# Four-pass window attention: masks that start before the score products are complete, and a new order of the PSUM copies

## Chip, core and metric

One core of one Trainium2 chip. The metric is the device time of one execution of the whole program in microseconds, the median of the runs taken.

## The reference, cut to what matters

The program is a chain of four layers over activations of 4 sequences x 1024 positions x 256 channels: a linear attention, a block of two local-attention layers with their feed-forward parts, a gated attention, and a ternary-weight feed-forward. The block of two layers stands in the program twice, so its attention part runs four times ("passes", `run` = 0 to 3). The change touches only this part:

```python
h = shift_token(x)                       # half of the channels one position later
q, k, v = split(h @ wqkv, 3)             # 8 heads of 64
q = l2norm(q) * qs;  k = l2norm(k) * ksc
q, k = rotary_xpos(q, k)
sim = q_window @ k_window^T              # 128 queries against their own and the previous 128 keys
sim = where(mask, -max, sim);  attn = softmax(sim)
x = x + (attn @ v_window) @ wo
```

## The kernel before

**Tiles and slots.** A pass works on 32 tiles of 128 positions (NT = 32). It is a software pipeline: in slot T each engine does its part of several tiles at once. T+3 is loaded, transposed and multiplied with the q and k weights, T+2 with the v weights, q and k of T+1 are turned (transposed) for the scores, T itself goes through scores, masks, exponentials and the transposition of the probabilities, T-1 through the products with V, T-2 through the output projection. The order of the steps within a slot is written out by hand for each engine in its function `slot`. Four slots (u = T mod 4) make an iteration; the first and last iterations are unrolled and the middle ones are a hardware loop. Engines are tied together by counting semaphores alone: every step waits for a count and adds one.

**TensorE** (`slot`, line 567): `sc_` (32 small score products in eight rounds, L508), `pv_` of T-1 (L544), `wo_` of T-2, `tr_` q of T+1 (four transposes, L478), `v_` of T+2 (six products, L363 to L365), `ht` of T+3 (two transposes, L419 and L420), `pt_` of two groups of heads (L521 to L523), `tr_` k of T+1 (L478), `qk_` q of T+3, two more `pt_`, `qk_` k of T+3.

**ScalarE** (`slot`, line 1264): the square of k (L1224), eight exponentials with row sums (`sc_`, L1247), the copy `OT_hi` of the numerator of T-1 (`ot_`, L1262), then the copies out of PSUM: qT (L1238), V (L1231), hT_hi (L1217), two probT (L1255), kT (L1238), the square of q, two more probT.

**VectorE** (`slot`, line 1921): the sum of squares of q (L1867), eight masks with running minimum (`sc_`, L1893, one per head, announced once for each pair of heads), the reciprocal of the first four sums (L1900), the rotation of k (L1853 to L1855), the second reciprocal, the normalising of k of the next tile (`norm_`, L1873), hT_lo (L1833), the sum of squares of k, `OT_lo` (L1905), the residual (L1910), the rotation of q.

**GpSimd** (`slot`, line 2718): the sums of the rotated halves (L2693), four products of probabilities with reciprocals (`pn_`, L2699), the inverse root of the norms (`pow_`, L2684 and L2686).

**SyncE** issues the loads of H (of tile T+4), the copies of V's halves and the stores; it is not changed.

**PSUM.** Banks 0 and 1 take q and k of T+3, bank 1 also the transposes of H; bank 5 takes v of T+2 and then the turned k of T+1, so the turning of k waits until ScalarE has copied V. Banks 2 to 4 are the scores and then the turned probabilities; banks 6 and 7 (`pair_bank`) the numerators in their lower halves, the projection in the upper half of bank 7.

The lines the reasons touch: `ht` waits for the reader of bank 1 (`k_read`, L417 and L418), `tr_` for V (`v_read(T + 1)`, in the branch of j = 1), `qk_` of T+3 for hT_lo (`s_dvHT`). In run 0 VectorE and GpSimd also normalise the residual stream of later tiles in the slots u = 1 to 3 (`extra`).

Of the kernel before, what the change touches and what calls it, by code (L numbers as in the profile page):

```python
# [94 lines left out]
def build(nc, a, out):  # L95

    ctx = ExitStack()
    with ctx:
# [169 lines left out]
        def gate_weight(x, i, n=1):  # L268
# [32 lines left out]
        s_dvQN, s_peS, s_peSB = sem("s_dvQN"), sem("s_peS"), sem("s_peSB")  # L301
# [22 lines left out]
                      *s_acKT, s_peS, s_peSB, *s_dvMX, *s_acEX, *s_plPN, *s_pePT, *s_acPT, *s_pePV, *s_dvRS,  # L324
# [12 lines left out]
        def input_bank(run, T):  # L337
            return bank[2 + T] if spare(run, T) else bank[1]
# [11 lines left out]
        def tensor_program(e):  # L350
# [36 lines left out]
            def pass_A(run, ffn_first):  # L387
# [25 lines left out]
                def ht(T, u):  # L413
# [3 lines left out]
                    if not spare(run, T) and not (isinstance(T, int) and T == 0):  # L417
                        k_read(T - 1)  # L418
# [13 lines left out]
                def qk_(T, u, j):  # L432
# [48 lines left out]
                def sc_(T, u):  # L481
# [7 lines left out]
                    for n, (odd, even, piece) in enumerate(SCORE_ORDER):  # L489
# [3 lines left out]
                        for half_ in range(2):  # L493
                            for h in (odd, even):
# [31 lines left out]
                def pv_(T, u):  # L526
# [18 lines left out]
                    for hf in range(2):  # L545
                        for x in (2, 3):
                            for g in range(2):
                                for i in range(2):
                                    product(2 * hf + g, i, x, slice(DH * i, DH * i + DH), hf == 0 and x == 2)
                    for hf in range(2):  # L550
                        for i in range(2):
                            for x in (0, 1):
                                for g in range(2):
                                    ins = product(2 * hf + g, i, x, slice(0, P), False)
                        ins.then_inc(s_pePV[hf], 1)
# [11 lines left out]
                def slot(T, u):  # L567
# [2841 lines left out]
```

## Time and profile before

| what | us |
|---|---|
| median of 3 runs | 3214.93 (3213.61 to 3220.47) |
| the profiled execution's own time | 3218.03 |
| its span, first to last instruction | 3216.0 |
| TensorE matmul busy | 3018.5 (94%) |
| VectorE busy | 2361.8 (73%) |
| ScalarE busy | 1721.1 (54%) |
| GpSimd busy | 1671.5 (52%) |
| granted TensorE clock, mean | 0.993 |

A busy matmul is counted from its start to its modelled end, and matmuls overlap, so TensorE's 94% hides waits: they are seen as steps between the starts of instructions. The four attention passes take about 390 us each.

### The profile page before, as it was taken

The page shows a single profiled execution, that of the slowest core. Times are in us where ns is not written, and L with a number is a line of the kernel's source. Part 1 is how long each engine was busy: PE and PEld are TensorE (multiplying, and loading weights), DVE is VectorE, ACT ScalarE, POOL GpSimd, SP SyncE. Part 2 cuts the span into 40 slices and gives each one's busy share as a digit, 9 for nine tenths or more (in the row PEclk, how much of TensorE's full clock was granted, in tenths as well). Part 3 has the DMA queues.
Part 4 walks back from the last instruction along what each step waited for, and adds up shares of the span by engine and source line. Part 5 has one row for each costly group of instructions (what it writes and reads, how often), then busy time and mean ns, then how long its engine had stood idle before and what let it go on. Part 6 is the DMA issues. An engine that isn't in the chain of part 4 may idle for free.

```text
span 3216.0 us, 98899 instructions
## 1 busy us (share of the span) xinstructions
PE 3018.5 (94%) x35586; PEld 2604.5 (81%) x35586; DVE 2361.8 (73%) x6543; ACT 1721.1 (54%) x4532; POOL 1671.5 (52%) x1839
## 2 busy tenths in 40 slices
PE   6999989989999999999899999999999899999889
PEld 4777878878887888998688878877888788898778
DVE  6777777677777786777677777767777688777766
ACT  4666652266667324665676763237666622454445
POOL 7777740077777224323777771037777444317610
PEclk9999999999999999999999999999999999999999
DMA  4211121021111101000211112102111200100001
GB/s 146 58 42 39 38 81 36 23 62 39 37 38 37 45 20 42 10 11 21 57 39 37 38 37 78 29 25 66 37 38 35 66 26 13 27 1 1 1 14 39
DMA packets 178773, 122.82 MB, mean 38 GB/s; under 512 B 27532, under 2 KB 175336, under 8 KB 178024
## 3 DMA queue, kind: packets, MB, share of 16 engines
q1 hardware_dynamic: 177432, 117.77, 13.6%
q8 instruction: 147, 2.41, 0.3%
q10 hardware_dynamic: 1104, 1.90, 0.2%
q14 instruction: 90, 0.74, 0.1%
HBM read 48.29 MB, written 20.98 MB: 22 GB/s over the span
## 4 chain that ended last, share of the span: by engine, by line
PE 62%; ACT 18%; issue 8%; DVE 8%; DMA 1%; POOL 1%; DVEq 1%; SPq 0%; ACTq 0%; POOLq 0%
ACT prob L1247 14%; PE bank L363 7%; PE bank L365 5%; PE scores L508 5%; PE bank L364 5%; PE scores L363 4%; PE scores L364 4%; PE scores L365 4%; PE bank L478 2%; PE pair_bank L770 2%; PE pair_bank L769 2%; PE pair_bank L768 2%; ACT V L1231 2%; PE scores L714 2%; PE scores L713 2%
## 5 line engine op out<-in xcount | busy, mean ns | idle before, releaser
L2699 POOL TENSOR_TENSOR prob<-prob,rsum 128x384 f32<-128x384 f32 x512 | 467.5, 933 | 282.6 <-DVE rsum L1900 267.2
L1247 ACT ACTIVATE prob<-prob,nmax 128x192 f32<-128x192 f32 x1024 | 452.0, 443 | 290.5 <-DVE nmax L1893 290.4
L1440 ACT ACTIVATE gate<-scores,bias 128x512 f32<-128x512 f32 x192 | 132.2, 689 | 511.4 <-PE scores L365 511.4
L2686 POOL TENSOR_TENSOR rn<-ss,mhalf 128x16 f32<-128x16 f32 x128 | 375.2, 2931 | 10.7
L363 PE MATMUL bank<-wqkv_hi,hT_hi 128*128 128x512 f32 x768 | 338.9, 441 | 8.7 <-DVE hT_lo L1833 3.7
L2693 POOL TENSOR_TENSOR qk<-rot_t 128x512 f32<-128x512 f32 x256 | 322.6, 1278 | 36.1 <-DVE ss L1867 29.7
L2667 POOL TENSOR_TENSOR rstd<-meanvar,eps 128x4 f32<-128x4 f32 x48 | 11.1, 231 | 627.2 <-DVE meanvar L1825 627.2
L1893 DVE CUSTOM_DVE_ANT_0 prob<-scores,masks,rn 128x192 f32<-128x192 f32 x768 | 267.7, 412 | 84.4 <-PE scores L508 83.9
L365 PE MATMUL bank<-wqkv_hi,hT_lo 128*128 128x512 f32 x768 | 305.7, 398 | 0.0
L364 PE MATMUL bank<-wqkv_lo,hT_hi 128*128 128x512 f32 x768 | 302.5, 394 | 0.0
L1853 DVE TENSOR_TENSOR rot_t<-bank,rot 128x512 f32<-128x512 f32 x256 | 176.1, 688 | 163.8 <-ACT qk L1224 156.2
L1224 ACT ACTIVATE qk<-bank 128x512 f32<-128x512 f32 x256 | 152.5, 597 | 221.8 <-PE bank L365 221.8
L363 PE MATMUL scores<-gT_hi,w_hi 128*128 128x512 f32 x576 | 227.5, 395 | 2.5 <-issue 1.7
L508 PEld LDWEIGHTS scores<-kT,qT 64*64 64x64 f32 x8192 | 184.6, 134 | 53.3 <-issue 53.3
L364 PE MATMUL scores<-gT_lo,w_hi 128*128 128x512 f32 x576 | 226.3, 393 | 0.0
L1255 ACT ACTIVATE probT<-scores 128x384 f32<-128x384 f32 x512 | 222.0, 488 | 6.2 <-PE scores L523 6.0
L365 PE MATMUL scores<-gT_hi,w_lo 128*128 128x512 f32 x576 | 224.3, 389 | 0.0
L478 PE MATMUL bank<-misc,qk 128*128 128x128 f32 x1024 | 158.3, 277 | 64.2 <-ACT V L1231 53.9
L508 PE MATMUL scores<-kT,qT 64*64 64x128 f32 (+1 forms) x8192 | 202.0, 248 | 8.3 <-ACT probT L1255 8.3
L363 PEld LDWEIGHTS bank<-wqkv_hi,hT_hi 128*128 128x128 f32 x768 | 145.6, 190 | 57.3 <-DVE hT_lo L1833 29.9
L1247 ACT ACTIVATION_READ_ACCUMULATOR prob<-prob,nmax 128x1 f32 x1024 | 191.5, 187 | 0.0
L478 PEld LDWEIGHTS bank<-misc,qk 128*128 128x128 f32 x1024 | 112.9, 141 | 92.9 <-DVE qk L1873 74.6
(338 smaller groups left out, 9662.6 us busy)
## 6 DMA issues: line engine op xcount, KB each, us to landing
Vlo<-V SPq DMA_DIRECT2D x256, 64.0 KB, 2.0
Vhi<-V SPq DMA_DIRECT2D x256, 64.0 KB, 2.0
H<-Y SPq DMA_DIRECT2D x128, 64.0 KB, 1.8
H<-ya SPq DMA_DIRECT2D x128, 64.0 KB, 1.9
yb<-Y SPq DMA_DIRECT2D x128, 64.0 KB, 1.6
HB<-Y SPq DMA_DIRECT2D x32, 256.0 KB, 2.8
HB<-yb SPq DMA_DIRECT2D x32, 256.0 KB, 3.0
raw<-in_L_ffn_wqkv SPq DMA_DIRECT2D x4, 1536.0 KB, 6.9
```

The costliest lines, as they stand in the source:

```text
L363: e.matmul(o, lh, rh, start=start, stop=False)
L364: e.matmul(o, lh, rl, start=False, stop=False)
L365: return e.matmul(o, ll, rh, start=False, stop=stop)
L478: i = e.transpose(o[:, c * P:(c + 1) * P], half(u, j)[:, c * P:(c + 1) * P], identf)
L508: ins = e.matmul(o, queries, keys, start=opens, stop=True, skip_group_check=True)
L1247: ins = e.activation(pb, pb, ACT.Exp, bias=nm[r][:, x:x + 1], scale=-1.0, accum_out=sums[r][:, x:x + 1])
L1255: e.activation(PTs[gi][:, :], b_[:, 0:2 * KW], ACT.Copy).then_inc(s_acPT[gi], 1)
L1853: e.tensor_tensor(o1_, x_, tab(2 * j, 0, DH), ALU.mult)
L1893: ins = e.tensor_tensor_reduce(Pb[gi][:, w], scores[:, s0:s0 + KW], m[:, DH:] if i == 0 else m[:, 0:KW], rn[u][:, h:h + 1], BIG, ALU.add, ...
L2686: e.tensor_tensor(rn[u][:, :], ss[:, :], mhalf[:, :], ALU.pow).then_inc(s_plRN, 1)
L2693: e.tensor_tensor(half(u, j), t1[:, w], t2[:, w], ALU.add).then_inc(s_plAD[j], 1)
L2699: e.tensor_tensor(pair, pair, rs[:, 2 * gi:2 * gi + 2].unsqueeze(2).to_broadcast([P, 2, KW]), ALU.mult).then_inc(s_plPN[gi], 1)
```

## The change

It touches the attention pass in six ways.

1. Heads are grouped anew (PAIRS, TURN_BANK), and a new semaphore `s_peSA` tells of the fifth of eight score rounds. VectorE masks heads 4 and 6 after that signal, then waits for the whole of the scores (`s_peS`) and masks the other six. All four waits for the turned probabilities (`s_pePT`) now stand ahead of the first mask. Each mask is announced by itself, and ScalarE's exponentials wait for a single mask each.
2. ScalarE's copy of the numerator (`ot_`) moves from behind the exponentials to behind kT, so qT, V, hT and two probT come ahead of it.
3. TensorE transposes H (`ht`) ahead of the turning of q and of v, not behind them, and into the unused upper half of bank 6. The wait for the reader of bank 1 moves from `ht` to the product of k (`qk_`, j = 1). `pv_` and ScalarE's `ot_` get a wait for hT_lo (`s_dvHT`), since bank 6 is shared.
4. VectorE normalises k of T+1 right behind the first reciprocal, ahead of the rotation of k and of the second reciprocal.
5. The groups of heads are turned, scaled and multiplied in the order 0, 1, 2, 3; `s_pePV[n]` now stands for groups n and n+2, with the waits to match.
6. GpSimd's waits on the masks count two for each tile.

```diff
-PAIRS = [(0, 4), (1, 5), (2, 6), (3, 7)]
+PAIRS = [(0, 4), (2, 6), (1, 5), (3, 7)]
+EXP_ORDER = (((0, 1), (1, 1), (0, 0), (1, 0)), ((2, 0), (3, 0), (2, 1), (3, 1)))
-TURN_BANK = (3, 2, 2, 4)
+TURN_BANK = (2, 3, 4, 2)
@@ input_bank
-            return bank[2 + T] if spare(run, T) else bank[1]
+            if spare(run, T):
+                return bank[2 + T]
+            return bank[1] if isinstance(T, int) and T < 3 else bank[6][:, 2 * P:4 * P]
@@ TensorE, ht and qk_
-                    if not spare(run, T) and not (isinstance(T, int) and T == 0):
+                    if run == DEPTH and isinstance(T, int) and 1 <= T < 3:
                         k_read(T - 1)
-                    elif j == 1 and spare(run, T):
+                    elif j == 1 and (not early or spare(run, T)):
                         k_read(T - 1)
@@ TensorE, sc_
+                                if half_ == 1 and h == 0 and piece == 0:
+                                    ins.then_inc(s_peSA, 1)
@@ TensorE, pt_
-                    if gi == 1:
-                        e.wait_ge(s_dvMX[2], G + 1 + OFF)
-                    if gi == 2:
-                        e.wait_ge(s_acPT[1], G + 1 + OFF)
+                    if gi == 0:
+                        e.wait_ge(s_dvMX[2], 2 * G + 2 + OFF)
+                        e.wait_ge(s_dvMX[3], 2 * G + 2 + OFF)
+                    if gi == 3:
+                        e.wait_ge(s_acPT[0], G + 1 + OFF)
@@ TensorE, pv_
+                    if inside(T + 3):
+                        e.wait_ge(s_dvHT, G + 4 + OFF)
@@ TensorE, slot
+                    if inside(T + 3):
+                        ht(T + 3, (u + 3) % U)
                     if inside(T + 1):
                         tr_(T + 1, (u + 1) % U, 0)
                     if inside(T + 2):
                         v_(T + 2, (u + 2) % U)
-                    if inside(T + 3):
-                        ht(T + 3, (u + 3) % U)
                     if inside(T):
+                        pt_(T, u, 0)
                         pt_(T, u, 1)
-                        pt_(T, u, 0)
@@ ScalarE, sc_
-                    e.wait_ge(s_dvMX[gi], G + 1 + OFF)
-                    for i in range(2):
+                    for n, (gi, i) in enumerate(EXP_ORDER[hf]):
                         x = 2 * gi + i
                         pb = Pb[gi][:, i * KW:(i + 1) * KW]
-                        ins = e.activation(pb, pb, ACT.Exp, bias=nm[r][:, x:x + 1], scale=-1.0, accum_out=sums[r][:, x:x + 1])
-                    ins.then_inc(s_acEX[gi], 1)
+                        e.wait_ge(s_dvMX[gi], 2 * G + 1 + n // 2 + OFF)
+                        e.activation(pb, pb, ACT.Exp, bias=nm[r][:, x:x + 1], scale=-1.0, accum_out=sums[r][:, x:x + 1]).then_inc(s_acEX[gi], 1)
@@ ScalarE, ot_
+                    if inside(T + 4):
+                        e.wait_ge(s_dvHT, G + 5 + OFF)
@@ ScalarE, slot
-                    if inside(T - 1):
-                        ot_(T - 1, (u - 1) % U)
                     if inside(T + 1):
                         tr_(T + 1, (u + 1) % U, 0)
...
                     if inside(T + 1):
                         tr_(T + 1, (u + 1) % U, 1)
+                    if inside(T - 1):
+                        ot_(T - 1, (u - 1) % U)
@@ VectorE, sc_
-                    e.wait_ge(s_peS, G + 1 + OFF)
+                    e.wait_ge(s_peSA, G + 1 + OFF)
                     e.sem_inc(s_passed, 1)
                     e.wait_ge(s_plRN, 2 * G + 2 + OFF)
                     e.sem_inc(s_passed, 1)
-                    e.wait_ge(s_pePT[gi], G + OFF)
-                    e.sem_inc(s_passed, 1)
+                    for g in range(NG):
+                        e.wait_ge(s_pePT[g], G + OFF)
+                        e.sem_inc(s_passed, 1)
...
-                    for i in range(2):
+                    for n, (gi, i) in enumerate(EXP_ORDER[0] + EXP_ORDER[1]):
+                        if n == 2:
+                            e.wait_ge(s_peS, G + 1 + OFF)
+                            e.sem_inc(s_passed, 1)
@@ VectorE, slot
                         rs_(T, u, 0)
+                    if inside(T + 1):
+                        norm_(T + 1, (u + 1) % U, 1)
                     if inside(T + 2):
                         qk_(T + 2, (u + 2) % U, 1)
                     if inside(T):
                         rs_(T, u, 1)
-                    if inside(T + 1):
-                        norm_(T + 1, (u + 1) % U, 1)
```

## Rows read from the trace of the kernel before

**Rows 1.** Windows, one slot each: us, busy by engine (count), clock, DMA share, GB/s

```profile
858.06:870.78 12.72, 12.12 (x182) 10.00 (x181) 9.05 (x32) 8.52 (x27) 9.19 (x9) 1.00 0.15 36
895.38:907.69 12.31, 11.75 (x181) 9.91 (x180) 9.09 (x32) 8.52 (x27) 9.38 (x9) 1.00 0.16 37
270.12:283.63 13.51, 11.94 (x182) 9.93 (x181) 11.24 (x36) 8.52 (x27) 10.08 (x10) 1.00 0.21 53
```

**Rows 2.** Waits, whole span: waiter <- releaser, us in total, times, longest

```profile
PE bank L478 <- ACT V L1231: 53.9, 115, 0.8
...
PE bank L419 <- DVE rot_t L1855: 30.0, 40, 4.3
PEld bank L363 <- DVE hT_lo L1833: 29.9, 117, 0.7
```

**Rows 3.** Timeline of TensorE: start, us, what, xcount, idle before

```profile
845.76 1.57 PE L508 MATMUL scores<-kT,qT 64*64 64x128 f32 x64
847.16 0.34 PE L544 MATMUL pair_bank<-probT,Vlo 64*64 64x64 f32 x8
...
851.97 0.40 PE L365 MATMUL bank<-wqkv_hi,hT_lo 128*128 128x512 f32 x1
852.21 0.28 PE L419 MATMUL bank<-misc,H 128*128 128x128 f32 x1
...
852.43 0.27 PE L521 MATMUL scores<-misc,prob 128*128 128x128 f32 x1
...
853.80 0.63 PE L478 MATMUL bank<-misc,qk 128*128 128x128 f32 x4 [0.55 <-ACT V L1231]
854.43 0.50 PE L363 MATMUL bank<-wqkv_hi,hT_hi 128*128 128x512 f32 x1
...
858.06 1.57 PE L508 MATMUL scores<-kT,qT 64*64 64x128 f32 x64
859.69 0.34 PE L544 MATMUL pair_bank<-probT,Vlo 64*64 64x64 f32 x8
...
872.28 0.34 PE L544 MATMUL pair_bank<-probT,Vlo 64*64 64x64 f32 x8
```

**Rows 4.** Timeline of ScalarE, the same slot

```profile
848.59 0.46 ACT L1247 ACTIVATE prob<-prob,nmax 128x192 f32<-128x192 f32 x1 [2.12 <-DVE nmax L1893]
...
852.12 0.58 ACT L1262 ACTIVATE OT_hi<-pair_bank 128x512 fp32r<-128x512 f32 x1
852.60 0.58 ACT L1238 ACTIVATE qT<-bank 128x512 f32<-128x512 f32 x1
853.07 0.58 ACT L1231 ACTIVATE V<-bank 128x512 f32<-128x512 f32 x1
853.55 0.37 ACT L1217 ACTIVATE hT_hi<-bank 128x256 fp32r<-128x256 f32 x1
...
854.55 0.60 ACT L1238 ACTIVATE kT<-bank 128x512 f32<-128x512 f32 x1
856.12 0.60 ACT L1224 ACTIVATE qk<-bank 128x512 f32<-128x512 f32 x1 [0.96 <-PE bank L365]
```

**Rows 5.** Chain of waits ahead of the first mask, the same slot (DVEq: VectorE's queue)

```profile
847.40 0.02 DVEq L1880
...
847.52 0.02 DVEq L1882
...
847.79 0.23 DVE prob L1893
```

**Rows 6.** Timeline of VectorE and GpSimd, the same slot

```profile
850.50 0.17 DVE L1900 RECIPROCAL rsum<-sums 128x4 f32<-128x4 f32 x1
...
852.43 0.69 DVE L1873 TENSOR_TENSOR qk<-qk,rn 128x512 f32<-128x512 f32 x1
...
850.75 0.83 POOL L2699 TENSOR_TENSOR prob<-prob,rsum 128x384 f32<-128x384 f32 x1 [2.17 <-DVE rsum L1900]
...
852.50 1.30 POOL L2699 TENSOR_TENSOR prob<-prob,rsum 128x384 f32<-128x384 f32 x1
```

More of the change, by code:

```diff
@@ L544, in product @@
                         return e.matmul(bank[6 + i][cols, o0:o0 + DH], keys[x][rows, h * DH:(h + 1) * DH], PTs[gi][rows, p0:p0 + DH], start=start, stop=x < 2, skip_group_check=True)
-                    for hf in range(2):
+                    for n in range(2):
                         for x in (2, 3):
-                            for g in range(2):
+                            for gi in (n, n + 2):
                                 for i in range(2):
-                                    product(2 * hf + g, i, x, slice(DH * i, DH * i + DH), hf == 0 and x == 2)
-                    for hf in range(2):
+                                    product(gi, i, x, slice(DH * i, DH * i + DH), n == 0 and x == 2)
+                    for n in range(2):
                         for i in range(2):
                             for x in (0, 1):
-                                for g in range(2):
-                                    ins = product(2 * hf + g, i, x, slice(0, P), False)
-                        ins.then_inc(s_pePV[hf], 1)
+                                for gi in (n, n + 2):
+                                    ins = product(gi, i, x, slice(0, P), False)
+                        ins.then_inc(s_pePV[n], 1)
                 def wo_(T, u):
@@ L587, in slot @@
                     if inside(T):
+                        pt_(T, u, 2)
                         pt_(T, u, 3)
-                        pt_(T, u, 2)
                     if inside(T + 3):
@@ L1253, in pt_ @@
                     e.wait_ge(s_pePT[gi], G + 1 + OFF)
-                    e.wait_ge(s_pePV[gi // 2], G + OFF)
+                    e.wait_ge(s_pePV[gi % 2], G + OFF)
                     e.activation(PTs[gi][:, :], b_[:, 0:2 * KW], ACT.Copy).then_inc(s_acPT[gi], 1)
@@ L1267, in slot @@
                     if inside(T):
+                        sc_(T, u, 0)
                         sc_(T, u, 1)
-                        sc_(T, u, 0)
-                        sc_(T, u, 3)
-                        sc_(T, u, 2)
-                    if inside(T - 1):
-                        ot_(T - 1, (u - 1) % U)
                     if inside(T + 1):
@@ L1287, in slot @@
                     if inside(T):
+                        pt_(T, u, 2)
                         pt_(T, u, 3)
-                        pt_(T, u, 2)
                 def iteration(it):
@@ L1873, in norm_, with sc_ @@
                     e.tensor_tensor(heads(half(u, j)), heads(half(u, j)), rn[u][:, j * HEADS:(j + 1) * HEADS].unsqueeze(2).to_broadcast([P, HEADS, DH]), ALU.mult).then_inc(s_dvQN, 1)
-                def sc_(T, u, gi):
+                def sc_(T, u):
                     G = R0 + T
@@ L1892, in sc_ @@
                         s0 = SCORE_AT[h]
-                        ins = e.tensor_tensor_reduce(Pb[gi][:, w], scores[:, s0:s0 + KW], m[:, DH:] if i == 0 else m[:, 0:KW], rn[u][:, h:h + 1], BIG, ALU.add, ALU.min, nm[r][:, x:x + 1])
-                    ins.then_inc(s_dvMX[gi], 1)
+                        e.tensor_tensor_reduce(Pb[gi][:, w], scores[:, s0:s0 + KW], m[:, DH:] if i == 0 else m[:, 0:KW], rn[u][:, h:h + 1], BIG, ALU.add, ALU.min, nm[r][:, x:x + 1]).then_inc(s_dvMX[gi], 1)
                 def rs_(T, u, hf):
                     G = R0 + T
-                    e.wait_ge(s_acEX[2 * hf], G + 1 + OFF)
-                    e.wait_ge(s_acEX[2 * hf + 1], G + 1 + OFF)
+                    e.wait_ge(s_acEX[2 * hf], 2 * G + 2 + OFF)
+                    e.wait_ge(s_acEX[2 * hf + 1], 2 * G + 2 + OFF)
                     e.reciprocal(rs[:, 4 * hf:4 * hf + 4], sums[u % 2][:, 4 * hf:4 * hf + 4]).then_inc(s_dvRS[hf], 1)
@@ L2680, in pow_ @@
                     e.wait_ge(s_dvSS[1], G + 1 + OFF)
-                    e.wait_ge(s_dvMX[2], G - 3 + OFF)
-                    e.wait_ge(s_dvMX[3], G - 3 + OFF)
+                    e.wait_ge(s_dvMX[2], 2 * G - 6 + OFF)
+                    e.wait_ge(s_dvMX[3], 2 * G - 6 + OFF)
                     e.sem_inc(s_passed, 1)
@@ L2701, in mask_of @@
                 def mask_of(it):
-                    e.wait_ge(s_dvMX[2], NT * run + U * it - U + 1 + OFF)
-                    e.wait_ge(s_dvMX[3], NT * run + U * it - U + 1 + OFF)
+                    e.wait_ge(s_dvMX[2], 2 * (NT * run + U * it - U + 1) + OFF)
+                    e.wait_ge(s_dvMX[3], 2 * (NT * run + U * it - U + 1) + OFF)
                     odd = it - 2 * (it // 2)
@@ L2723, in slot @@
                     if inside(T):
+                        pn_(T, u, 0)
                         pn_(T, u, 1)
-                        pn_(T, u, 0)
+                        pn_(T, u, 2)
                         pn_(T, u, 3)
-                        pn_(T, u, 2)
                     if inside(T + 2):
```

13 lines of the change are left out of this document (5 added, 8 removed).

## The prediction

> **What bounds the kernel now.** Start with the slot, since the change touches nothing else. The windows give its length: 12.72 us where it is the first of an iteration (u = 0), 12.31 in the others, 13.51 where run 0 has extra VectorE work in it [rows 1]. The clock is at its upper level in all three, so it is no part of the sum. Then the waits. TensorE's turning of k waits for ScalarE's copy of V in 115 slots, 53.9 us in all; its product of q waits for hT_lo in 117, 29.9 us in all; and the transposes of H wait 40 times for VectorE's rotation of k, 30.0 us in all [rows 2]. Last the timelines, which say why. I count from the start of the scores at 845.76. TensorE starts the last product of v at 6.21, the transposes of H at 6.45, the first turned probabilities at 6.67, and then stands 0.55 before the turning of k at 8.04; the product of q follows at 8.67 and the next scores at 12.30 [rows 3]. ScalarE begins its exponentials at 2.83, is through after 3.53 and copies the numerator, qT, V and hT, each 0.48 apart: V at 7.31 [rows 4]. The last product of v ended at 6.21 + 0.40 = 6.61, so **V lay finished in PSUM for 0.70 us while ScalarE was at earlier work.** That queue, not TensorE, sets the slot: scores, masks, exponentials, numerator, qT, V, then TensorE again.
>
> **The parts, one by one,** for this slot (u = 3).
>
> *Numerator copy behind kT.* V needs only the exponentials and qT before it: 2.83 + 3.53 + 0.48 = 6.84, which is 0.48 earlier, with the masks as they are.
>
> *H ahead of q and v.* Its two transposes cost TensorE 0.22 wherever they stand (852.21 to 852.43 [rows 3]). In front of v they delay it by this: the last product of v ends at 6.61 + 0.22 = 6.83, and V can start at 6.86, with 0.03 for the signal. So both ends meet: V moves from 7.31 to 6.86, **0.45 earlier**, and from there TensorE's own order sets it.
>
> *What follows V follows unchanged.* The turning of k starts 0.73 behind V's copy, the product of q 1.36 behind it (through hT and hT_lo, which stay behind V on ScalarE), the next scores 3.63 after that [rows 3, 4]: 6.86 + 1.36 + 3.63 = 11.85. I take 11.86. TensorE still stands some 0.28 before the turning of k (7.59, against 7.00 + 0.33 for the end of its work) and 0.27 before q.
>
> *Early masks.* The five rounds end three eighths of 1.40 us (845.76 to 847.16 [rows 3]) before the rest: 0.53. But VectorE's queue steps through its waits 0.12 apart [rows 5], and three more of them now stand ahead of the first mask: 0.35 back. The first mask moves from 2.03 to 1.85. Eight masks take 2.71 (847.79 to 850.50 [rows 5, 6]), 0.34 each, and the exponentials now wait for one, not two: 1.85 + 0.34 + 0.12 = 2.31 against 2.83. ScalarE is ready for V at 6.32, and V is not there until 6.86. **In the plain slots this part buys nothing but 0.52 of reserve.** If that cover were gone (signal no earlier, all waits in series) the first exponential would come at 2.84, as now, still no loss on this path.
>
> *Normalising k earlier.* It takes 0.69 and now starts about when GpSimd starts its first product of probabilities. One that met it in the trace took 1.30, one that did not 0.83 [rows 6]. The first reciprocal comes at 1.85 + 2.71 = 4.56, GpSimd 0.25 later at 4.81 [rows 6], the second product ends at 4.81 + 1.30 + 0.83 = 6.94. TensorE wants it at 6.67 + 0.22 + 0.11 = 7.00 and could have it as late as 7.2 without loss, since the turning of k waits for V until 7.59. No cost, but only 0.3 of slack. The rotation of k and the second reciprocal move 0.60 back: the rotation takes at most the 1.58 between the two reciprocals, so the second is out by 4.56 + 0.17 + 0.60 + 1.58 = 6.91, and the last two products end by 6.91 + 0.25 + 1.66 = 8.8; TensorE wants the first of them behind the product of q, at 8.22 + 1.5 = 9.7. Hidden. The trace thus prices the meeting at 0.47. The Trainium skill (SBUF — State Buffer, Who interferes with whom) says more: a VectorE instruction with two SBUF inputs and a GpSimd one that reads SBUF block each other fully. By that rule the second product would end near 7.1 in a plain slot and some 0.06 too late in a u = 0 slot, 2 us in all, so 3163 rather than 3161; it speaks against this part of the change, and the trace agrees in kind.
>
> *New waits.* Those of `pv_` and `ot_` for hT_lo are met long before: hT_lo is made right behind V. Behind ScalarE's `ot_` stands the square of q. kT starts 1.48 behind V (8.34), the numerator at 8.82, done at 9.4; the square is due 1.69 behind the product of q, at 9.91 [rows 3, 4]. 0.5 of slack. The wait for bank 1's reader sits at the product of k, at about 10.3, and the rotation it waits for is over by 6.9. The second wait for the scores is met while the first two masks run. SyncE's order of DMAs is unchanged; its stores come behind the residual, about 0.3 later, and nothing in the slot waits for them.
>
> *u = 0 and u = 1.* With u = 0 the products with V start 1.63 after the scores (858.06, 859.69), with u = 1 1.50 (870.78, 872.28), else 1.40 [rows 1, 3]. Those 0.23 and 0.10 lay under ScalarE's queue and now come out: 12.09 and 11.96. The u = 0 slot is 0.41 longer today because its masks start that much later; now its exponentials start at 2.72 and the reserve swallows that. Its transposes of H no longer wait for the rotation either. Gains: 0.63 for u = 0, 0.34 for u = 1 (taken as 12.30 before), 0.45 for u = 2 and 3, mean 0.47.
>
> *Run 0.* About ten slots like the one of 13.51 have masks 1.20 late or somewhat less. There V is not the limit any more but the products of probabilities: first mask 3.23, second product at 3.23 + 2.96 + 1.30 + 0.83 = 8.32, the turning of k 1.1 later than in the plain slot, slot about 13.0. The gain is 0.5 or, with the extra waits in series, 0.35: as in the others.
>
> **The sum.** 115 slots with this wait [rows 2] x 0.47 = 54 us. First and last slots of the passes have other limits; I count them at nothing, at most 13 x 0.5 = 6 us more. The profiled execution took 3218.03, so 3164; the median of the runs stands 3.1 below it, so 3214.93 - 54 = **3161**. Bounds: the share of the 0.70 that comes out cannot be above 0.99 a slot (all of TensorE's standing: 0.72 + 0.27), and the smallest with the order as it is would be the 0.2 of the first rival.
>
> **Rivals.**
> - *Probabilities become the limit (smaller gain).* If the early signal gains nothing against its waits (first mask at 2.03 + 0.35 = 2.38) the second product ends at 7.47 and TensorE turns k at 7.85, not 7.59: slot 12.1, gain 0.2, 23 us: 3192. For it: slack of only 0.3, and the waits in series [rows 5]. Against: three of eight rounds are surely behind the signal.
> - *More comes out.* If the turning of k follows V's end (0.59) with no 0.14 on top, since TensorE's queue arrives early, 0.14 x 115 = 16 us more: 3145.
> - *No change.* The 0.55 is a wait for something else that only ends with V. Then 3215. Against: V's copy and this wait end together in 115 slots [rows 2].
> - *Slower.* The numerator copy now stands ahead of the square of q on ScalarE. It decides once kT comes more than 0.5 late (the two probT copies before it hang on GpSimd's products): the square, the rotation of q and the next masks then slip; 0.52 of reserve in the masks goes next; beyond 1.0 each slot grows, beyond 1.46 it is longer than today, and at 2.0 by 0.54: 62 us, 3277. For that the product beside the normalising would have to take over 3 us, not 1.30.
>
> **Chances.** Forecast 0.70; smaller gain 0.14; more 0.09; no change 0.04; slower 0.03. The forecast's own range is 3150 to 3172 (0.37 to 0.56 a slot). To hold eight in ten it has to reach most of the second and third cases: 3143 to 3190. A measurement tells 0.2%, 6.4 us, from no change: faster 0.93, same 0.04, slower 0.03.
>
> **What the profile would show.** Right: plain slots of about 11.86; V's copy starting as the last product of v ends, at 6.9 after the scores; ScalarE idle some 0.5 between qT and V; first mask near 1.85; the first product of probabilities at 1.30 and the third at 0.83. Wrong: a wait of TensorE's L521 for GpSimd's L2699 in plain slots (first rival), VectorE's rotation of q waiting on a late square (the last), or slots still at 12.3.

## The result, and the profile after

The changed kernel takes 3183.07 us (median of 4 runs, 3181.24 to 3185.26); the kernel before took 3217.70 beside it (4 runs, 3213.61 to 3222.32). The ratio is 0.9892 (0.9875 to 0.9910): **34.6 us faster, where 54 were forecast** (3161, range 3143 to 3190). The profiled execution took 3181.24, its span is 3179.4 (3216.0 before).

The page of the changed kernel, busy time and the chain that ended last (on this chain TensorE had 62% and ScalarE 18% before):

```profile
PE 3021.5 (95%) x35586; PEld 2610.9 (82%) x35586; DVE 2342.6 (74%) x6543; ACT 1739.8 (55%) x4532; POOL 1654.2 (52%) x1839
...
PE 80%; DVE 8%; issue 4%; ACT 3%; POOL 2%; SPq 2%; DMA 1%; DVEq 0%; ACTq 0%; POOLq 0%
```

Windows of the changed kernel, one slot each (us, busy by engine, clock, DMA share, GB/s): a plain slot, one with u = 0, one with u = 1, and one of run 0 with u = 2. They answer to [rows 1]:

```profile
830.67:842.67 12.00, 11.86 (x181) 10.06 (x180) 8.89 (x32) 8.68 (x27) 9.21 (x9) 1.00 0.16 38
842.67:855.08 12.41, 11.94 (x182) 10.06 (x181) 8.89 (x32) 8.68 (x27) 9.19 (x9) 1.00 0.15 37
855.08:867.17 12.09, 11.91 (x181) 10.06 (x180) 8.78 (x31) 8.69 (x27) 9.19 (x9) 1.00 0.16 37
...
263.11:275.78 12.67, 11.89 (x182) 9.98 (x181) 11.01 (x36) 8.60 (x27) 9.71 (x10) 1.00 0.22 56
```

The plain slot fell by 0.31, u = 0 by 0.31, u = 1 by some 0.2, the slot of run 0 by 0.84. The clock is at its upper level in all, as before. From the first scores of each pass to the start of its last slot's scores, the four passes together fell from 1543.1 to 1500.0; all that lies outside this, the last slot of each pass (T = 31) included, grew from 1672.9 to 1679.4. Below, "in the slots" and "outside the slots" mean these two. So 43.1 came out of the slots and 6.5 were given back elsewhere.

Waits of the changed kernel, whole span (waiter <- releaser, us in total, times, longest), beside [rows 2]:

```profile
ACT V L1239 <- PE bank L368: 66.1, 109, 2.6
...
PEld scores L527 <- POOL prob L2706: 51.5, 61, 5.6
...
PEld bank L366 <- DVE hT_lo L1840: 26.7, 101, 0.8
```

The direction turned round: ScalarE's copy of V now waits for TensorE's last product of v, 109 times, where before V lay finished in PSUM. The waits of the transposes of H for the rotation are gone. TensorE's waits for GpSimd's products of probabilities are not in the plain slots: they stand mostly in the first two and last two slots of the passes (up to 5.2 in a first slot, 1.9 to 3.0 in the last ones) and in the slots of run 0 with extra work. Those on the row of the matmuls (PE L527) are 39 us in all, where the same wait was 10 in the kernel before.

Timeline of the changed kernel: TensorE in the plain slot at 830.67 and in the u = 0 slot at 842.67, then ScalarE, VectorE and GpSimd in the plain slot, and ScalarE's V with u = 0. It answers to [rows 3, 4, 6]:

```profile
830.67 1.57 PE L511 MATMUL scores<-kT,qT 64*64 64x128 f32 x64
832.18 0.34 PE L552 MATMUL pair_bank<-probT,Vlo 64*64 64x64 f32 x8
...
837.21 0.39 PE L368 MATMUL bank<-wqkv_hi,hT_lo 128*128 128x512 f32 x1
837.44 0.27 PE L527 MATMUL scores<-misc,prob 128*128 128x128 f32 x1
...
838.39 0.63 PE L481 MATMUL bank<-misc,qk 128*128 128x128 f32 x4
839.03 0.50 PE L366 MATMUL bank<-wqkv_hi,hT_hi 128*128 128x512 f32 x1
...
844.45 0.34 PE L552 MATMUL pair_bank<-probT,Vlo 64*64 64x64 f32 x8 [0.21 <-issue]
...
849.48 0.40 PE L368 MATMUL bank<-wqkv_hi,hT_lo 128*128 128x512 f32 x1
...
833.05 0.46 ACT L1255 ACTIVATE prob<-prob,nmax 128x192 f32<-128x192 f32 x1 [1.67 <-DVE nmax L1904]
...
837.64 0.60 ACT L1239 ACTIVATE V<-bank 128x512 f32<-128x512 f32 x1 [0.49 <-PE bank L368]
...
839.62 0.65 ACT L1271 ACTIVATE OT_hi<-pair_bank 128x512 fp32r<-128x512 f32 x1
840.73 0.60 ACT L1232 ACTIVATE qk<-bank 128x512 f32<-128x512 f32 x1 [0.46 <-PE bank L368]
...
850.05 0.60 ACT L1239 ACTIVATE V<-bank 128x512 f32<-128x512 f32 x1 [0.48 <-PE bank L368]
...
832.59 0.42 DVE L1904 CUSTOM_DVE_ANT_0 prob<-scores,masks,rn 128x192 f32<-128x192 f32 x1 [0.65 <-issue]
...
835.39 0.66 DVE L1880 TENSOR_TENSOR qk<-qk,rn 128x512 f32<-128x512 f32 x1
...
835.55 1.19 POOL L2706 TENSOR_TENSOR prob<-prob,rsum 128x384 f32<-128x384 f32 x1 [1.85 <-DVE rsum L1910]
...
836.70 0.82 POOL L2706 TENSOR_TENSOR prob<-prob,rsum 128x384 f32<-128x384 f32 x1
```

Counted from the scores, forecast in brackets: products with V 1.51 (1.40), first mask 1.92 (1.85), exponentials 2.38 (2.31), last product of v 6.54 (6.43), V 6.97 (6.86), turning of k 7.72 (7.59), product of q 8.36 (8.22), numerator 8.95 (8.82), next scores 12.00 (11.86). ScalarE stands 0.49 ahead of V, as said. **On TensorE every step is where it was forecast but for one shift of about 0.11, which is already there at the products with V** and is handed down to the end, where it has become 0.14. (Masks and exponentials are 0.07 late as well, which V does not feel: ScalarE stands idle ahead of it.) What shifted them is the first question; the second is the u = 0 slot (12.41, forecast 12.09); the third is the 6.5 us outside the slots.

### The profile page after: what moved, and what is told of

Its sections match the earlier page's. It is cut to its first block, busy times and chain, and to the rows that moved or that the text cites. A ratio compares the mean times of both kernels' runs of the same rounds, so it can differ in the third digit from the quotient of the medians.

```text
span 3179.4 us, 98692 instructions
## 1 busy us (share of the span) xinstructions
PE 3021.5 (95%) x35586; PEld 2610.9 (82%) x35586; DVE 2342.6 (74%) x6543; ACT 1739.8 (55%) x4532; POOL 1654.2 (52%) x1839
## 4 chain that ended last, share of the span: by engine, by line
PE 80%; DVE 8%; issue 4%; ACT 3%; POOL 2%; SPq 2%; DMA 1%; DVEq 0%; ACTq 0%; POOLq 0%
PE bank L366 8%; PE bank L368 7%; PE bank L367 6%; PE pair_bank L552 6%; PE scores L511 5%; PE scores L366 4%; PE scores L367 4%; PE scores L368 4%; PE bank L481 3%; PE pair_bank L778 2%; PE pair_bank L777 2%; PE pair_bank L776 2%; PE pair_bank L366 2%; PE scores L722 2%; PE scores L721 2%
## 5 line engine op out<-in xcount | busy, mean ns | idle before, releaser
L2706 POOL TENSOR_TENSOR prob<-prob,rsum 128x384 f32<-128x384 f32 x512 | 451.8, 910 | 244.3 <-DVE rsum L1910 244.3
L2693 POOL TENSOR_TENSOR rn<-ss,mhalf 128x16 f32<-128x16 f32 x128 | 375.3, 2932 | 10.6
L1874 DVE TENSOR_REDUCE ss<-qk 128x8 f32<-128x512 f32 x256 | 173.4, 679 | 24.7 <-POOL rn L2693 21.8
L527 PE MATMUL scores<-misc,prob 128*128 128x128 f32 x512 | 146.0, 285 | 39.8 <-POOL prob L2706 38.8
```

The source lines that it names most:

```text
L2693: e.tensor_tensor(rn[u][:, :], ss[:, :], mhalf[:, :], ALU.pow).then_inc(s_plRN, 1)
L2706: e.tensor_tensor(pair, pair, rs[:, 2 * gi:2 * gi + 2].unsqueeze(2).to_broadcast([P, 2, KW]), ALU.mult).then_inc(s_plPN[gi], 1)
```

## The experiments

Diffs are against the changed kernel unless said, and show the lines that matter. The first four share 3214.97 for the kernel before, the next four 3216.98, the last two 3217.45. "Plain slot" is one with u = 2 or 3 in pass 1; a mean is that of six.

**1. The wait in `pv_` taken out.** The theory: a wait that is already met still takes a step in TensorE's queue, and the products with V are the first instruction with nothing in front to cover it. The count it waits for was already waited for by the product of q in the slot before, so the order of the work stays as safe without it.

```diff
@@ TensorE, pv_
-                    if inside(T + 3):
-                        e.wait_ge(s_dvHT, G + 4 + OFF)
```

> The changed kernel without the wait for hT_lo in TensorE's pv_ (TensorE has waited for the same count one slot earlier, in its product of q). Theory Q (TensorE's own queue sets the slot now, and the tenth wait ahead of the products with V costs 0.11 us there): those products start 1.40 us after the scores in plain slots, not 1.51, the plain slot is 11.89 instead of 12.00, and the whole 12 us shorter, about 3171. Rival P (the products of probabilities, or ScalarE behind the late numerator copy, set the slot): the products with V start earlier and a wait elsewhere takes the 0.11; slot 12.00, time within 3 us of the changed kernel's 3183.

3175.17 us (3173.70 to 3178.95), ratio 0.9878 (0.9862 to 0.9895): 8 less than the change, where 12 less were expected. Windows of a plain slot and a u = 0 slot, and the timeline, of this kernel:

```profile
829.56:841.46 11.90, 11.76 (x181) 10.01 (x180) 8.89 (x32) 8.68 (x27) 9.20 (x9) 1.00 0.16 38
841.46:853.71 12.25, 12.06 (x182) 10.06 (x181) 8.88 (x32) 8.68 (x27) 9.18 (x9) 1.00 0.15 37
```

```profile
829.56 1.57 PE L511 MATMUL scores<-kT,qT 64*64 64x128 f32 x64
830.96 0.34 PE L550 MATMUL pair_bank<-probT,Vlo 64*64 64x64 f32 x8
...
836.42 0.60 ACT L1237 ACTIVATE V<-bank 128x512 f32<-128x512 f32 x1 [0.39 <-PE bank L368]
```

The products with V are back at 1.40 and V at 6.86, the forecast's own numbers, and the slot is 11.90 (forecast 11.86). Over the slots T = 8 to 28 of passes 1 to 3 the mean length fell by 0.12, from 12.12 to 12.00. The slots of run 0 with extra work kept theirs (12.67, and 12.71 here), since they are bound otherwise; that is part of why 8 us came out and not 12.

**2. H back behind v,** into bank 1, with the waits of the kernel before.

```diff
@@ TensorE, slot (and input_bank, the bank 1 waits, the two s_dvHT waits as before)
-                    if inside(T + 3):
-                        ht(T + 3, (u + 3) % U)
                     if inside(T + 1):
                         tr_(T + 1, (u + 1) % U, 0)
                     if inside(T + 2):
                         v_(T + 2, (u + 2) % U)
+                    if inside(T + 3):
+                        ht(T + 3, (u + 3) % U)
```

> The changed kernel with H transposed behind the product of v again, into bank 1, and without the two waits for hT_lo that bank 6 needs. Theory Q: V's copy starts at 6.64 after the scores instead of 6.97, all behind it follows, plain slot 11.67, u = 0 slots about 12.2; in all some 0.3 x 115 = 34 us less than the changed kernel, 3149. Rival P: V is copied earlier but the turning of k waits for the turned probabilities, which wait for GpSimd; slot 11.9 to 12.0, 3175 to 3183.

3168.21 us (3164.55 to 3169.80), ratio 0.9849 (0.9833 to 0.9866): 15 less than the change. Its plain slot is 11.76. Timeline of the slot at 831.05:

```profile
837.84 0.30 PE L420 MATMUL bank<-misc,H 128*128 128x128 f32 x1 [0.18 <-DVE rot_t L1856]
...
837.70 0.60 ACT L1235 ACTIVATE V<-bank 128x512 f32<-128x512 f32 x1 [0.17 <-PE bank L366]
```

V comes at 6.65, 0.32 earlier than in the change. But H waits for the rotation of k (6.79), hT and hT_lo with it, and the product of q starts at 8.13: 0.23 earlier, not 0.32. Since this kernel has no wait in `pv_` either, its fair partner is number 1: plain slot 11.90 there, 11.76 here, 7 us in all. So H ahead of v does take away the wait for the rotation, as forecast, and costs more than it saves in the slots of passes 1 to 3.

In run 0 it is the other way round. Where VectorE's extra work makes the rotation late, H behind v waits longer, and the slot has 13.07, 0.40 more than in the change. Timeline of such a slot of this kernel (starts at 264.00):

```profile
272.09 0.30 PE L420 MATMUL bank<-misc,H 128*128 128x128 f32 x1 [1.49 <-DVE rot_t L1856]
```

The kernel came out 19 above the 3149 expected of it. The slots alone explain most of this: they gained 15.5 over the change, not 34, as a slot of passes 1 to 3 (T = 8 to 28) gained some 0.25, not 0.3, and the same 21 slots of run 0 gained 1.2 together. Outside the slots it takes 1683.5, 4.1 more than the change; why was not pursued.

**3. The numerator alone,** moved behind kT in the kernel before (diff against that).

```diff
@@ ScalarE, slot
-                    if inside(T - 1):
-                        ot_(T - 1, (u - 1) % U)
                     if inside(T + 1):
                         tr_(T + 1, (u + 1) % U, 0)
...
                     if inside(T + 1):
                         tr_(T + 1, (u + 1) % U, 1)
+                    if inside(T - 1):
+                        ot_(T - 1, (u - 1) % U)
```

> The kernel before with one step moved: ScalarE copies the numerator behind kT. Theory Q (the early masks buy nothing as long as the numerator copy is out of the way): V at 6.84 after the scores, plain slot 11.84, u = 0 slots 12.25, 0.46 x 115 = 53 us less than before, 3165, so faster than the whole change. Rival S (the gain needs both ScalarE parts, each alone gives half or less): plain slot 12.1 or more, 3195 or more.

3176.24 us (3172.31 to 3179.80), ratio 0.9878 (0.9861 to 0.9894). Windows of a plain and a u = 0 slot:

```profile
830.32:842.14 11.82, 11.73 (x181) 9.93 (x180) 9.16 (x32) 8.53 (x27) 9.34 (x9) 1.00 0.16 38
842.14:854.38 12.24, 11.91 (x181) 10.02 (x180) 9.13 (x31) 8.52 (x27) 9.19 (x9) 1.00 0.16 38
```

Slots as expected (11.84 and 12.25). **One step moved gives 0.48 of a plain slot, and the whole change 0.31.** The time is 11 above the 3165 expected, and the ratios of this kernel and of the change overlap (0.9861 to 0.9894, 0.9875 to 0.9910): that this kernel is the faster one is clear in the plain slots, not in the total. The two last slots before the end of each pass and what lies outside the slots (1677.6, 4.7 more than before) take back part of the gain.

**4. The masks alone:** the changed kernel with numerator and H where they were (waits as in experiment 2). One signal for each mask, the new order of the heads and the early normalising of k remain in it.

```diff
@@ ScalarE, slot (and TensorE's ht and input_bank as in experiment 2)
+                    if inside(T - 1):
+                        ot_(T - 1, (u - 1) % U)
                     if inside(T + 1):
                         tr_(T + 1, (u + 1) % U, 0)
...
-                    if inside(T - 1):
-                        ot_(T - 1, (u - 1) % U)
```

> The changed kernel with the numerator copy and the transposes of H both at their places of before: early masks, one signal for each mask, new order of the heads, and k normalised early remain. Theory Q (masks and numerator copy buy the same 0.45, either alone is enough): first exponential at 2.38, V at 6.87, plain slot 11.9, u = 0 slots 12.3, about 0.42 x 115 = 48 us less than before, 3170. Rival S: plain slot 12.1 or more, 3195 or more.

3158.18 us (3154.69 to 3160.66), ratio 0.9822 (0.9806 to 0.9839), 12 less than expected. The plain slot is 11.86, the u = 0 slot 12.27: early masks and a late numerator each take some 0.45 out of ScalarE's queue ahead of V. They do not add: number 2 has both, with H behind v, and its plain slot is 11.76, where two times 0.45 would give 11.4. V is then held by its own product, at 6.65.

This kernel is 18 faster than number 3 though its plain slots are no shorter. Half of that lies outside the slots: 1668.7 here, 1677.6 in number 3, 1679.4 in the change. The other half lies in the slots at the ends of the passes: the last two before T = 31 together take 7.2 less over the four passes, the first four 4.6 less. The kernels with the late numerator lose at the ends of the passes.

**5. The first mask waits for all scores,** the rest of the change kept.

```diff
@@ VectorE, sc_
-                    e.wait_ge(s_peSA, G + 1 + OFF)
+                    e.wait_ge(s_peS, G + 1 + OFF)
```

> The changed kernel with VectorE's first mask waiting for the whole of the scores (one signal for each mask stays). Theory Q (with the numerator copy out of the way the early masks are reserve): first mask at 2.45 after the scores instead of 1.92, V's copy stays at 6.97; only the products of probabilities become tight, plain slot 12.0 to 12.1, the whole 3183 to 3193. Rival M (the early masks carry the gain): V's copy and the slot move by 0.3 to 0.5, 3218 or more.

3185.89 us (3184.35 to 3186.82), ratio 0.9898 (0.9881 to 0.9916). Its plain slot at 833.97 has 11.99, as in the change, and ScalarE's timeline there shows:

```profile
840.33 0.58 ACT L1246 ACTIVATE qT<-bank 128x512 f32<-128x512 f32 x1
840.94 0.60 ACT L1239 ACTIVATE V<-bank 128x512 f32<-128x512 f32 x1
```

The first exponential comes at 2.83, 0.45 later than in the change, and V at the same 6.97. ScalarE's idle time ahead of V fell from some 0.5 to 0.04, so this reserve is all but used up. Beside the late numerator the early masks are reserve.

**6. Normalising k at its old place.**

```diff
@@ VectorE, slot
-                    if inside(T + 1):
-                        norm_(T + 1, (u + 1) % U, 1)
                     if inside(T + 2):
                         qk_(T + 2, (u + 2) % U, 1)
                     if inside(T):
                         rs_(T, u, 1)
+                    if inside(T + 1):
+                        norm_(T + 1, (u + 1) % U, 1)
```

> The changed kernel with the normalising of the next k behind the second reciprocal again, as before. Theory Q: it ends at about 6.95 after the scores, ahead of the turning of k at 7.72, and meets the third product of probabilities (1.2 to 1.3 us) instead of the first; plain slot stays 12.00; in the slots of run 0 with late masks the products come 0.35 sooner; in all 0 to 5 us less, 3178 to 3183. Rival N (the early normalising is worth something): plain slot 12.1 or more, 3193 or more.

3181.34 us (3179.08 to 3185.04), ratio 0.9885 (0.9865 to 0.9905): no difference from the change, and the plain slot is 11.99. In this kernel that part buys and costs nothing.

**7. The numerator at its old place in the last two slots of a pass only.**

```diff
@@ ScalarE, slot
+                def tail(T):
+                    return isinstance(T, int) and T > NT - 3
...
+                    if inside(T - 1) and tail(T):
+                        ot_(T - 1, (u - 1) % U)
                     if inside(T + 1):
                         tr_(T + 1, (u + 1) % U, 0)
...
-                    if inside(T - 1):
+                    if inside(T - 1) and not tail(T):
                         ot_(T - 1, (u - 1) % U)
```

> The changed kernel with the numerator copy at its place of before in the last slots of a pass alone (T of 30 and more), where no H is transposed any more. Theory T (in the last slots the late numerator copy holds VectorE's OT_lo, behind which the feed-forward's statistics and weight rounding stand, and these delay the masks of the last tile by 2 us): the middle slots stay as they are, each pass ends 1.5 to 2.5 us sooner, in all 6 to 10 us, 3175. Rival: the time outside the slots is lost elsewhere (at the starts), no change, 3183.

3168.42 us (3165.47 to 3170.95), ratio 0.9844 (0.9825 to 0.9863): 14.7 less than the change, and more than expected. The timeline at the end of pass 1, first the changed kernel (its last slot starts at 1020.50):

```profile
1019.52 0.69 DVE L1915 TENSOR_TENSOR OT_lo<-pair_bank,OT_hi 128x512 fp32r<-128x512 f32 x1 [2.77 <-ACT OT_hi L1271]
...
1023.03 1.49 DVE L2063 TENSOR_TENSOR w_lo<-raw,w_hi 128x1280 fp32r<-128x1280 f32 x1
1024.44 0.41 DVE L1904 CUSTOM_DVE_ANT_0 prob<-scores,masks,rn 128x192 f32<-128x192 f32 x1
...
1028.28 0.33 PE L527 MATMUL scores<-misc,prob 128*128 128x128 f32 x1 [2.87 <-POOL prob L2706]
```

and this one (its last slot starts at 1019.16):

```profile
1015.88 0.69 DVE L1920 TENSOR_TENSOR OT_lo<-pair_bank,OT_hi 128x512 fp32r<-128x512 f32 x1 [0.23 <-ACT OT_hi L1271]
...
1021.05 0.42 DVE L1909 CUSTOM_DVE_ANT_0 prob<-scores,masks,rn 128x192 f32<-128x192 f32 x1 [0.16 <-issue]
...
1024.89 0.33 PE L527 MATMUL scores<-misc,prob 128*128 128x128 f32 x1 [0.97 <-POOL prob L2711]
```

In the last slots VectorE has, behind OT_lo and the residual, the statistics and the rounding of weights for the next stage, and only then the masks. A numerator that comes late pushes all of it: the first mask is at 3.94 in the changed kernel and at 1.89 here, and TensorE's gap ahead of the turned probabilities is 2.87 against 0.97. The other three passes show the same 3.94 and 1.89; the kernel before had 2.00, 2.00, 2.36 and 2.00. That is 2.05 in each of four passes, 8.2 in all. The profiled executions of the two kernels differ by 11.8, of which 10.6 lie outside the slots; the 2.4 between 8.2 and 10.6 were not followed.

**8. Combined.** Numbers 1 and 7, and the room behind v used: TensorE turns q behind v, so that this lies inside the copy of V, and ScalarE copies hT, V, qT in that order, V's waits reduced to one met early and then the signal of the product.

```diff
@@ TensorE, slot
-                    if inside(T + 1):
-                        tr_(T + 1, (u + 1) % U, 0)
                     if inside(T + 2):
                         v_(T + 2, (u + 2) % U)
+                    if inside(T + 1):
+                        tr_(T + 1, (u + 1) % U, 0)
@@ ScalarE, v_
-                    e.wait_ge(s_peV, G + 1 + OFF)
-                    e.wait_ge(s_pePV[0], G - 2 + OFF)
                     e.wait_ge(s_pePV[1], G - 2 + OFF)
+                    e.wait_ge(s_peV, G + 1 + OFF)
@@ ScalarE, slot
-                    if inside(T + 1):
-                        tr_(T + 1, (u + 1) % U, 0)
-                    if inside(T + 2):
-                        v_(T + 2, (u + 2) % U)
                     if inside(T + 3):
                         ht(T + 3, (u + 3) % U)
+                    if inside(T + 2):
+                        v_(T + 2, (u + 2) % U)
+                    if inside(T + 1):
+                        tr_(T + 1, (u + 1) % U, 0)
```

> A combination: the changed kernel without pv_'s wait; ScalarE copies hT, then V, then qT; V's wait for the products of the tile before stands ahead of the wait for V; TensorE turns q behind the product of v, so that this lies in the wait for V's copy; numerator copy at the old place in the last slots. Theory Q: V's copy starts 0.43 after the start of the last product of v, at 6.50 after the scores; TensorE's work up to the turning of k ends at 7.40, later than V's copy and its 0.75, and the product of q follows without a wait for hT_lo; plain slot 11.4 to 11.5, the whole about 3112. Rival P (VectorE's rotation and sum, or GpSimd's products and inverse root, hold the slot at once): 11.7 or more, 3140 or more.

3113.90 us (3109.40 to 3117.61), ratio 0.9672 (0.9653 to 0.9690): 103 us faster than before and 69 faster than the change. Windows of a plain and a u = 0 slot, and the timeline of the plain one (expected were 11.4 to 11.5 for it, and 3112):

```profile
857.25:868.59 11.34, 11.34 (x182) 10.05 (x181) 8.72 (x32) 8.68 (x27) 9.16 (x9) 1.00 0.17 40
868.59:880.26 11.67, 11.55 (x181) 10.02 (x180) 8.72 (x32) 8.68 (x27) 9.09 (x9) 1.00 0.16 39
```

```profile
863.27 0.39 PE L368 MATMUL bank<-wqkv_hi,hT_lo 128*128 128x512 f32 x1
863.50 0.60 PE L481 MATMUL bank<-misc,qk 128*128 128x128 f32 x4
863.94 0.27 PE L527 MATMUL scores<-misc,prob 128*128 128x128 f32 x1
...
864.59 0.60 PE L481 MATMUL bank<-misc,qk 128*128 128x128 f32 x4
864.99 0.47 PE L366 MATMUL bank<-wqkv_hi,hT_hi 128*128 128x512 f32 x1
...
863.76 0.60 ACT L1236 ACTIVATE V<-bank 128x512 f32<-128x512 f32 x1 [0.24 <-PE bank L368]
```

TensorE's busy time is the whole plain slot (11.34 of 11.34): it works while V is copied, k is turned at 7.34 without a stall and the product of q follows at 7.74. What each part of this kernel gives was not run alone. If numbers 1 and 7 give here the 8 and 15 that they gave by themselves, some 46 of the 69 are left for the new order; that is an estimate. That it needs the reserve that the change gave to ScalarE and VectorE is likely, but not shown: the new order was not tried on the kernel before.

**9. V's waits alone.** The second question, u = 0: in the changed kernel V starts 0.57 after its last product of v starts (849.48, 850.05), 0.43 in a plain slot (837.21, 837.64). The theory: behind TensorE's signal ScalarE's queue has two more waits, and with u = 0 a step on the register of the loop.

```diff
@@ ScalarE, v_
-                    e.wait_ge(s_peV, G + 1 + OFF)
-                    e.wait_ge(s_pePV[0], G - 2 + OFF)
                     e.wait_ge(s_pePV[1], G - 2 + OFF)
+                    e.wait_ge(s_peV, G + 1 + OFF)
```

> The changed kernel with one thing turned round on ScalarE: V's wait for the products of the tile before stands ahead of its wait for the product of v, and the first of the two counts, which the second implies, is left out. Theory W (in u = 0 slots ScalarE steps through these waits, and a register computation for them, between TensorE's signal and the copy): V's copy in u = 0 slots starts 0.43 after the start of the last product of v, not 0.57, those slots fall from 12.41 to 12.27, the others stay; 29 x 0.14 = 4 us, 3179. Rival: the 0.14 is something else of the loop's start; u = 0 slots stay at 12.41.

3185.31 us (3184.51 to 3186.17), ratio 0.9900 (0.9884 to 0.9917): not faster than the change, where 3179 was expected. Timeline, a plain slot (starts at 832.48) and a u = 0 slot (844.51):

```profile
839.00 0.40 PE L368 MATMUL bank<-wqkv_hi,hT_lo 128*128 128x512 f32 x1
...
851.26 0.40 PE L368 MATMUL bank<-wqkv_hi,hT_lo 128*128 128x512 f32 x1
...
839.50 0.60 ACT L1238 ACTIVATE V<-bank 128x512 f32<-128x512 f32 x1 [0.53 <-PE bank L368]
...
851.75 0.60 ACT L1238 ACTIVATE V<-bank 128x512 f32<-128x512 f32 x1 [0.34 <-PE bank L368]
```

V comes 0.49 behind in the u = 0 slot, down from 0.57, but 0.50 behind in the plain slot, up from 0.43. Over all slots T = 8 to 27 of passes 1 to 3 it is 0.49 to 0.50 in every one. The u = 0 slots fell by 0.07 in the mean (12.37 to 12.30; the one shown has 12.27), half of what was expected; the others grew by some 0.05 (12.11 to 12.16, and 12.01 to 12.05). So the waits do take part in the u = 0 slot's extra time, and the other three lose what it gains. Why the plain one got slower is open.

**10. VectorE's waits turned as well,** on top of number 8: the early signal is waited for last, not first (diff against number 8).

```diff
@@ VectorE, sc_
-                    e.wait_ge(s_peSA, G + 1 + OFF)
-                    e.sem_inc(s_passed, 1)
                     e.wait_ge(s_plRN, 2 * G + 2 + OFF)
...
+                    e.wait_ge(s_peSA, G + 1 + OFF)
+                    e.sem_inc(s_passed, 1)
```

> The combination of e8 with VectorE's wait for the early signal behind its other waits instead of ahead of them. Theory W: the first mask starts at 1.3 to 1.4 after the scores, not at 1.92. In plain slots TensorE is busy throughout, so they stay at 11.32; the u = 0 slots lose the 0.1 that they wait for the second product of probabilities; the last slots of each pass, which hang on these products, and the slots of run 0 with late masks gain some 0.1 to 0.5 each: 3106, between 3102 and 3111. Rival: the masks slow down or TensorE's last three rounds do, since both then work on the scores' banks; no gain or a loss, 3114 or more.

3110.63 us (3103.78 to 3114.72), ratio 0.9665 (0.9644 to 0.9686). In the timeline the first mask comes at 1.34 (slot at 841.50), against 1.92 with the signal first:

```profile
842.84 0.42 DVE L1906 CUSTOM_DVE_ANT_0 prob<-scores,masks,rn 128x192 f32<-128x192 f32 x1 [0.24 <-PE scores L511]
```

So the steps in the queue do eat the early signal, 0.58 of it. The time is 3.3 under that of number 8, within the spread of the runs. In the plain slots the masks are no limit any more: they have 11.3 in both kernels. The u = 0 slots fell from 11.68 to 11.60, as forecast, and the slots of run 0 with the latest masks from 12.49 to 12.19, so there the masks still count; 4.2 more outside the slots hid part of this.

## Why the prediction was right, and where it was not

**Right.** What bounds the kernel: ScalarE's queue, with V finished in PSUM. With the late numerator V came as its product ended, and the time fell, as the chain of waits had said. ScalarE's 0.5 of idle ahead of V, the early masks as mere reserve (number 5) and the normalising at no cost (number 6) stood. The new stacking of ScalarE's queue left the square of q on time (the rival on the slower side: OT_hi at 8.95, the square due at 10.06, and 0.46 idle between them). The slot of run 0 is bound by the products of probabilities, as said, first mask at 3.24 (3.23 forecast). TensorE in that slot of the changed kernel (starts at 263.11):

```profile
270.75 0.30 PE L527 MATMUL scores<-misc,prob 128*128 128x128 f32 x1 [0.73 <-POOL prob L2706]
```

**Wrong: "Those of `pv_` and `ot_` for hT_lo are met long before", counted at nothing.** The wait is met (TensorE waited for the same count a slot earlier), but its step in TensorE's queue is not covered: 0.11 in a plain slot, 8 us in all (number 1). The rest of the plain slot's miss, 0.03, is the way from V to the product of q: 1.39, not 1.36.

**Wrong: "now its exponentials start at 2.72 and the reserve swallows that", as the whole of the u = 0 slot.** Late masks are swallowed: the exponentials start at 2.83 there and ScalarE still stands idle ahead of V. But the products with V come at 1.78, not 1.63, and with them the last product of v at 6.81 for a forecast 6.66; V starts 0.57 behind that, not 0.43; and 0.03 are lost behind V as in the plain slot. 0.15, 0.14 and 0.03 make 12.41 out of 12.09. Number 1 shows that the wait in `pv_` is 0.09 of the first, number 9 that the waits ahead of V are 0.07 of the second; the rest of both is open. Both go with the start of an iteration of the hardware loop: in the u = 0 slot at T = 28, which is unrolled, the products with V come at 1.50, V 0.43 behind its product, and the slot has 11.99 to 12.00 in each pass.

**Wrong: "First and last slots of the passes have other limits; I count them at nothing".** Behind the late numerator VectorE's first mask in the last slot of a pass comes at 3.94, against some 2.0 before and 1.89 with the numerator early there. Undoing it there gives 14.7 (number 7). The prediction looked at what is queued behind the numerator in the middle of a pass (the square of q on ScalarE, the stores) and did not look at the ends, where statistics and weights stand between OT_lo and the masks. The first slots err the other way: they gained 12.9, more than the 6 that the prediction allowed for all first and last slots.

**The sum, remade.** These are the steps between the starts of slots, added up from the two profiled executions, beside 0.47 for each slot:

| slots | number | gained, us | at 0.47 each |
|---|---|---|---|
| T = 8 to 28, passes 1 to 3 | 63 | 18.6 | 29.6 |
| T = 8 to 28, run 0 | 21 | 9.0 | 9.9 |
| T = 4 to 7 | 16 | 0.3 | 7.5 |
| T = 29 and 30 | 8 | 2.3 | 3.8 |
| T = 0 to 3 | 16 | 12.9 | counted at nothing |
| outside the slots | | -6.5 | counted at nothing |

The sum is 36.6, the difference of the spans. The first row is what the misses above explain: u = 0 short by 0.29 in the mean, the others by some 0.15. In run 0 the slots of 13.51 gained 0.84 each for a forecast 0.5: the turning of k came 0.64 earlier, and the product of q now follows it by 0.45, where it was 0.63. Why T = 4 to 7 gained nothing and the first four so much was not followed.

**So the time lies in the range partly by luck.** Without the 12.9 of the first slots it would have been about 3196, beyond the 3190 that the range allowed.

The forecast's first rival gave nearly the measured size, 3192, by another mechanism: no TensorE wait for GpSimd's products stands in the plain slot. It stands in the slots of run 0 and at the ends of the passes. The meeting of normalising and product cost 1.19 - 0.82 = 0.37 (1.30 - 0.83 in the trace before), the second product ending at 6.85. The rule of the Trainium skill (SBUF — State Buffer, Who interferes with whom), by which the one that starts first holds the other up fully, was worked out in the prediction to an end near 7.1, an estimate. The two instructions overlap here by 0.50 (835.55 to 836.05) and 0.37 of it was lost, so the trace agrees in kind and the loss is somewhat smaller than a full block.

## What to carry to other kernels

When a change hands the bound from one engine's queue to TensorE's, price every wait that it adds to TensorE's queue, met or not: what nothing covers is paid in every slot that TensorE bounds. Two edits that take time out of the same queue ahead of the same copy do not add, so first ask what each does alone (here the masks alone gave 56.8 us, the numerator alone 38.7, both together with H 34.6; the first stands clear of the other two, these two are not clear of each other), and look at the last slots of a pass on their own, since other work stands behind the moved step there. What paid next here was work put inside the round trip of a copy out of PSUM (number 8, together with numbers 1 and 7).

## What the runs showed of the hardware

A semaphore wait that is long met cost TensorE 0.11 us where it was one more ahead of the products with V (1.51 with it, 1.40 without, number 1). VectorE's waits in series took 0.58 us off an early signal when they stood behind it, and not when they stood ahead of it (first mask at 1.92 in number 8, 1.34 in number 10). On ScalarE, dropping one of three waits ahead of a copy and waiting for the late one last gained 0.08 in one kind of slot and lost 0.07 in another (number 9). A copy of 128x512 out of PSUM between two TensorE instructions took 0.43 from the start of the last product to the start of the copy and 0.75 from there to the matmul that waits for it, 1.18 in all; in number 8 TensorE did 1.09 of other work in between (863.50 to 864.59).

When VectorE's normalising of k and a GpSimd product of probabilities meet, the one that starts later pays. In the changed kernel the normalising started first 122 times, took 0.66 and made the product 1.18 to 1.19 long, against 0.82 alone. In number 6, where the product started first and had 0.3 left (33 times), the product kept its 0.83 and the normalising took 0.84 in the mean, against 0.68 alone.
